# A selective scan with four convolutions: two packed tap matmuls, and u, z and dt sooner in the order

## The reference, cut to what matters

```
xz = einsum(x, in_proj_w); xi, z = split(xz)
xc = causal depthwise conv of xi over pixels, 4 taps
u = silu(xc + conv_b)
dt, B, C = split(einsum(u, x_proj_w)); delta = softplus(dt * dt_proj_w + b)
h = h * exp(delta * A) + delta * u * B        (one step per pixel, 16 states)
y = (h . C + u * D) * silu(z);  out = einsum(y, out_proj_w) + chunk
```

## Time and profile before

| | us |
|---|---|
| median of 3 runs | 8072.02 (8068.12 to 8075.87) |
| the profiled execution | 8083.31, of which the instructions span 8081.5 |
| TensorE busy | 6926.8 (86%) |
| VectorE busy | 6670.6 (83%) |
| ScalarE busy | 5321.7 (66%) |
| GpSimd busy | 5911.0 (73%) |

### The profile page before, as it was taken

One profiled execution on the slowest core, in us unless ns is written; L12 is line 12 of the kernel. 1 busy time (PEld: TensorE's weight loads), 2 busy tenths in 40 slices (PEclk: granted clock), 3 DMA queues, 4 the chain that ended last, 5 costly groups with the idle time before them and its releaser, 6 DMA issues. The chain is left out here.

```text
span 8081.5 us, 108343 instructions
## 1 busy us (share of the span) xinstructions
PE 6926.8 (86%) x31741; PEld 4163.9 (52%) x31741; DVE 6670.6 (83%) x9221; ACT 5321.7 (66%) x9423; POOL 5911.0 (73%) x5627
## 2 busy tenths in 40 slices
PE   8896877878888999999789999999789999996876
PEld 8893333333334555555435555555255555554665
DVE  6776989898989898999889999999898989894111
ACT  0135777777776778777777787777677787773221
POOL 0005989898988888888888888888888888884000
PEclk9998989898989999999989999999899999998999
DMA  9774666565667565656776566656865656565001
GB/s 169 166 179 123 179 166 180 166 178 163 181 173 191 162 164 159 164 165 162 184 194 169 159 166 163 165 157 164 208 172 162 167 159 166 161 164 137 2 2 32
DMA packets 1187366, 1261.38 MB, mean 156 GB/s; under 512 B 475904, under 2 KB 1172992, under 8 KB 1186816
## 3 DMA queue, kind: packets, MB, share of 16 engines
q1 hardware_dynamic: 950784, 1177.89, 54.9%
q10 hardware_dynamic: 236032, 77.08, 4.2%
HBM read 995.47 MB, written 181.59 MB: 146 GB/s over the span
## 5 line engine op out<-in xcount | busy, mean ns | idle before, releaser
L651 POOL TENSOR_TENSOR hs<-hs,bsp 128x448 f32<-128x448 f32 x3584 | 3718.2, 1059 | 411.5 <-DVE hs L641 401.2
L641 DVE TENSOR_TENSOR_SCAN hs<-da,hs,ps 128x448 f32<-128x448 f32 x3072 | 3491.6, 1137 | 0.0
L631 DVE TENSOR_TENSOR ps<-ps,bsp 128x448 f32<-128x448 f32 x3585 | 2200.3, 614 | 368.6 <-PE ps L615 367.9
L621 ACT ACTIVATE da<-da,nega 128x448 f32<-128x448 f32 x3588 | 2252.7, 661 | 51.5 <-issue 37.4
L856 PE MATMUL ps<-pv,ws 128*128 128x224 f32 x8800 | 1882.2, 359 | 218.1 <-DVE pv L920 122.4
L856 PEld LDWEIGHTS ps<-pv,ws 128*128 128x128 f32 x8800 | 1642.4, 190 | 502.3 <-DVE pv L920 202.7
L615 PE MATMUL ps<-stack,seld 96*128 96x448 bf16 x3587 | 1277.6, 370 | 349.4 <-DVE hs L641 260.9
L615 PEld LDWEIGHTS ps<-stack,seld 96*128 96x128 bf16 x3587 | 344.3, 98 | 1328.0 <-DVE hs L641 801.6
L920 DVE SCALAR_TENSOR_TENSOR pv<-ps,R 128x224 f32<-128x224 f32 x880 | 412.5, 469 | 734.6 <-PE ps L856 734.4
L662 PE MATMUL ps<-hs,wc 128*32 128x448 f32 x7200 | 964.2, 589 | 1.5 <-POOL hs L651 1.2
L422 PE MATMUL ps<-xn,wtap 128*128 128x448 f32 x1808 | 857.6, 577 | 9.7 <-ACT xn L526 9.7
(11 more groups left out here) (123 smaller groups left out, 8066.8 us busy)
## 6 DMA issues: line engine op xcount, KB each, us to landing
da<-delta_copy SPq DMA_DIRECT2D x3595, 224.0 KB, 3.8
stack<-parts SPq DMA_DIRECT2D x2700, 28.0 KB, 2.6
delta_copy<-dlt SPq DMA_DIRECT2D x225, 224.0 KB, 1.9
xin<-x_column_pairs SPq DMA_DIRECT2D x224, 145.0 KB, 3.5
x_column_pairs<-otile SPq DMA_DIRECT2D x225, 116.0 KB, 3.1
lnx<-in_x SPq DMA_DIRECT2D x115, 224.0 KB, 2.6
lny<-y_nchw SPq DMA_DIRECT2D x115, 224.0 KB, 2.8
xpad<-in_x SPq DMA_DIRECT2D x64, 392.0 KB, 7.1
```

Source lines behind the costliest of these rows:

```text
L621: a.activation(da[:, j % SLOTS, :], da[:, j % SLOTS, :], ACT.Exp, scale=nega[:, j:j + 1])\
L631: v.tensor_tensor(du, du, bsp[:, st.t % 2, 0, :], ALU.mult).then_inc(S["dbu_done"], 1)
L641: v.tensor_tensor_scan(hs[:, j, 1:T + 1], da[:, j % SLOTS, :], ps[:, DU_BANK + j % 4, 0:T], 0.0 if first else hs[:, j, T:T + 1], ALU.mult, ...
L651: g.tensor_tensor(hs[:, j, 0:T], hs[:, j, 1:T + 1], bsp[:, st.t % 2, 1, :], ALU.mult)\
```

## The change

The taps: `pack_pixels` (SyncE, two DMAs for each tile) copies the 64 rows of one image from xn into both halves of a new buffer xpack, the upper half one pixel further. One matmul then does two taps, so that `conv_tap` is two matmuls, and z reads xpack too. Its DMAs stand at unit 10 of SyncE, three tiles ahead, and wait for xn and for the reading of the buffer's last contents.

The order: on TensorE the taps end at unit 2, bc0 stands at 5 (before 6), dt at 6 (7), lnc at 7 (5), bc1 at 9 (8), lnv at 10 (9). On ScalarE silu's table, u, z and the other table stand at unit 4 (5), relu and cast0 behind them at 5 (4), bc0 at 6 (8), dt at 7 (9), lnc and cast1 at 8 (7), dt2 at 9, bc1 at 11, lnv at 12, clip at 13 (15). On GpSimd rest0 moves from 4 to 6, rest1 from 7 to 9, scale from 12 to 13, and delta_u from 15 to 14, ahead of the last product. The layer norm is done one tile sooner, and the last pair has none to prepare.

The blocks: one per tile, at unit 13 of TensorE, in a bank of the shared pair, read by VectorE at unit 15, loaded and stored at unit 5 of SyncE. Three are left for the tail. Steps are placed anew around them and no longer share a bank with blocks.

The rest: x3's borders are zeroed at the end of the second phase; work for tiles beyond the last is not issued.

```diff
-PE_AT = {0: ["tap0"], 1: ["last3", "tap1"], 2: ["tap2", "tap3"], 3: ["z"], 4: ["project"], 5: ["lnc"], 6: ["bc0"],
-         7: ["dt"], 8: ["sum0", "bc1"], 9: ["lnv"], 11: ["sum1"], 14: ["sum2"]}
+PE_AT = {0: ["tap0"], 1: ["last3"], 2: ["tap1"], 3: ["z"], 4: ["project"], 5: ["bc0"], 6: ["dt"], 7: ["lnc"],
+         8: ["sum0"], 9: ["bc1"], 10: ["lnv"], 11: ["sum1"], 13: ["blk"], 14: ["sum2"]}
 PE_US = {"tap": 0.9, "las": 0.95, "pro": 1.1, "z": 0.9, "lnc": 0.95, "lnv": 0.95, "bc0": 0.9, "bc1": 0.9, "dt": 0.9,
-         "sum": 0.95, "spread": 0.2, "skip": 0.9, "block": 2.25, "step": 1.9}
-ACT_AT = {0: ["prescale"], 4: ["relu", "cast0"], 5: ["silu", "u", "z", "exp"], 6: ["evacuate"], 7: ["lnc", "cast1"], 8: ["bc0"],
-          9: ["dt"], 10: ["dt2", "bc1"], 11: ["lnv"], 15: ["shift", "clip"]}
+         "sum": 0.95, "blk": 2.25, "spread": 0.2, "skip": 0.9, "block": 2.25, "step": 1.9}
+ACT_AT = {0: ["prescale"], 4: ["silu", "u", "z", "exp"], 5: ["relu", "cast0"], 6: ["evacuate", "bc0"], 7: ["dt"],
+          8: ["cast1", "lnc"], 9: ["dt2"], 11: ["bc1"], 12: ["lnv"], 13: ["clip"], 15: ["shift"]}
 DVE_AT = {3: ["gate"]}
-POOL_AT = {1: ["add_x"], 4: ["rest0"], 7: ["rest1"], 10: ["delta_log"], 12: ["scale"], 15: ["delta_u"]}
-SP_AT = {2: ["copy"], 8: ["part0"], 11: ["part1"], 13: ["part2"], 14: ["store"]}
+POOL_AT = {1: ["add_x"], 6: ["rest0"], 9: ["rest1"], 10: ["delta_log"], 13: ["scale"], 14: ["delta_u"]}
+SP_AT = {2: ["copy"], 8: ["part0"], 11: ["part1"], 10: ["pack"], 13: ["part2"], 14: ["store"]}
...
-            wtap = sb(m, "wtap", [P, 2, 4, P])
+            wtap = sb(m, "wtap", [P, 2, P])
+            xpack = sb(m, "xpack", [P, 2, T + 2])
...
-                self.has_ln = t < 4 or t >= 11
-                self.ln = p * KT + (t + 3 if t < 4 else t - 4)
-                self.ln_k = t + 3 if t < 4 else t - 11
-                self.ln_pair = p if t < 4 else (p + 1) % PAIRS
+                self.far_u = UB[ft]
+                soon, late = (3 if p else 4), ST - 4
+                self.has_ln = t < soon or t >= late and p + 1 < PAIRS
+                self.ln_pair = p if t < soon else (p + 1) % PAIRS
+                self.ln_k = t + KT - soon if t < soon else t - late
+                self.ln = self.ln_pair * KT + self.ln_k
...
+        FAR = ("tap0", "tap1", "u", "z", "dt", "dt2", "delta_log", "clip", "delta_u")
+        NEXT = ("bc0", "bc1", "cast0", "cast1", "rest0", "rest1", "copy", "part0", "part1", "part2")
+
+        def stands(st, name):
+
+            if name in FAR:
+                return st.far < TILES
+            if name in NEXT:
+                return st.next < TILES
+            return st.has_ln or name not in ("lnc", "lnv", "prescale", "relu", "shift", "add_x", "scale")
...
+                if name == "blk":
+                    if not BLOCKS_LEFT or tile < tile_of(*BLOCKS_LEFT[0]) + 2:
+                        continue
+                    BLOCK_AT[tile] = BLOCKS_LEFT.pop(0)
+                    TASK_LIST.append((name, BLOCK_NO[BLOCK_AT[tile]]))
+                elif not stands(st, name):
...
+            if back == "blk":
+                pe.wait_ge(D["cv_evac"], n + 2)
...
-                pe.wait_ge(S["xn_ready"], st.far_xn)
-            a = st.far_k * T + k
-            mm = pe.matmul(ps[:, TMP_BANK + bank, 0:T], wtap[:, st.far_s, k, :], xn[:, a:a + T],
-                           start=(k == 0), stop=(k == 3))
-            if k == 3:
+                pe.wait_ge(packed[st.far % 2], st.far // 2 * 32 + 32)
+            mm = pe.matmul(ps[:, TMP_BANK + bank, 0:T], wtap[:, k, :], xpack[:, st.far % 2, 2 * k:2 * k + T],
+                           start=(k == 0), stop=(k == 1))
+            if k == 1:
                 mm.then_inc(S["tmp_done"], 1)
+
+        def pack_pixels(sp, tile):
+
+            if tile >= 2:
+                sp.wait_ge(S["tmp_done"], Z_DONE[tile - 2])
+            s, k = tile % ST // KT, tile % KT
+            sp.wait_ge(S["xn_ready"], tile // ST * KT + k + 1)
+            for shift in range(2):
+                sp.dma_start(xpack[C * shift:C * shift + C, tile % 2, :],
+                             xn[C * s:C * s + C, k * T + shift:k * T + shift + T + 2]).then_inc(packed[tile % 2], 16)
...
-                    return pe.matmul(o, wcs("gate_in", st.far_s, P), xn[:, a:a + T], start=True, stop=True)
+                    return pe.matmul(o, wcs("gate_in", 0, P), xpack[:, st.far % 2, 2:T + 2], start=True, stop=True)
...
-            tail = []
-            for g in range(GROUPS):
-                for b in sorted(range(BLOCKS), key=lambda b: (tile_of(g, b), b)):
-                    ready = (tile_of(g, b) + 2) * UN + 8
-                    if ready > last - 4:
-                        tail.append(("block", g, b))
-                    else:
-                        place(("block", g, b), range(ready, min(ready + 16, last)))
...
+            with sp.Fori(0, PAIRS - 1) as i:
+                for b in range(2):
+                    sp.wait_ge(sa["split"], i * 2 + (b + 1))
+                    load_x(i + 1, b)
+            barrier(sp, 1)
...
             sp.wait_ge(D["zeroed"], 1)
             blank = hs[:, :, :].rearrange("p n f -> p (n f)")
             for rows in (0, H + 1):
                 sp.dma_start(x3[0:N, :, rows, :].rearrange("n p w -> p n w"),
...
-            sp.wait_ge(D["x3_zeroed"], 32)
-            barrier(sp, 1)
...
+                        if j == 5 and st.tile in BLOCK_AT:
+                            load_block(sp, *BLOCK_AT[st.tile])
+                        if j == 5 and st.tile - 1 in BLOCK_AT:
+                            keep_block(sp, *BLOCK_AT[st.tile - 1])
...
+                            elif name == "pack":
+                                if st.tile + 3 < TILES:
+                                    pack_pixels(sp, st.tile + 3)
...
+                            elif name == "blk":
+                                if st.tile in BLOCK_AT:
+                                    wait_bank(pe, st, name)
+                                    conv_block(pe, *BLOCK_AT[st.tile], TMP_BANK + BANK_NO[(st.tile, name)] % 2)
...
-            for s in range(2):
-                for k in range(4):
-                    ins = v.tensor_tensor(wtap[:, s, k, :], wps("conv_in", s, P), wps("taps", k, P), ALU.mult)
+            for k in range(2):
+                v.tensor_tensor(wtap[:, k, :], wps("conv_in", 0, P), wps("taps", k, P), ALU.mult)
...
+            v.wait_ge(D["x3_zeroed"], 32)
...
+                        if j == 15 and st.tile in BLOCK_AT:
+                            block_out(v, *BLOCK_AT[st.tile], TMP_BANK + BANK_NO[(st.tile, "blk")] % 2)
```

More of the change, by code:

```diff
@@ L726, in last_of @@
             return 55 * (d + 1)
[L728 removed]
+        LATE = {"dve": 2, "act": 6, "first": -3, "load": -8}
         FETCH, STEPS_FROM = 4 * UN, 6 * UN + 4
[L731 to L734 removed]
         def pe_work():
             out = []
[L739 removed]
+            for tile in range(TILES):
                 for j in range(UN):
@@ L840, in conv_block, with conv_step @@
             mm.then_inc(D["cv_done"], 1)
-        def conv_step(pe, G, m, alone=False):
+        def conv_step(pe, G, m):
             d = direction(m)
-            if not alone and PREVIOUS[("step", G, m)][0] == "block":
-                bank_free(pe, ("step", G, m))
             if m == last_of(d) - 54 + (d >= 2):
@@ L1073, in _ @@
             store(sp, tile, par, N - 1, k)
-            for j in range(LEAD["load"]):
-                sp.wait_ge(spread_in[j], (PAIRS * ST + 1) * 16)
-            for n in range(TILES * UN - LATE["keep"], TILES * UN):
-                if n in EV_AT and EV_AT[n][0] == "block":
-                    keep_block(sp, EV_AT[n][1], EV_AT[n][2])
+            keep_block(sp, *BLOCK_AT[TILES - 1])
             sp.wait_ge(S["y_summed"], TILES * 4 + 4)
-            sp.wait_ge(S["exp_done"], TILES * UN + LEAD["decay"] + 2)
             for k in range(NB):
@@ L1152, in _ @@
                     for j in range(UN):
-                        spread_du(pe, *unit(st, j + LEAD["du"]))
+                        if st.tile * UN + j + LEAD["du"] < TILES * UN:
+                            spread_du(pe, *unit(st, j + LEAD["du"]))
                         for name in PE_AT.get(j, ()):
+                            if not stands(st, name):
+                                continue
                             if name == "project":
@@ L1276, in _ @@
                     for j in range(UN):
-                        decay(a, *unit(st, j + LEAD["decay"]))
+                        if st.tile * UN + j + LEAD["decay"] < TILES * UN:
+                            decay(a, *unit(st, j + LEAD["decay"]))
                         for name in ACT_AT.get(j, ()):
+                            if not stands(st, name):
+                                continue
                             if name == "silu":
@@ L1305, in _ @@
                         e = event_at(st.tile, j, LATE["act"])
-                        if e is not None and e[0] == "step":
+                        if e is not None:
```

(3 more changed lines are left out.)

181 lines of the change are left out of this document (78 added, 103 removed).

## The result

The changed kernel is slower: 8348.22 us median (8340.72 to 8351.75, 4 runs) against 8073.94 of the kernel before beside it; the ratio is 1.0339 with a 95% interval of 1.0326 to 1.0352. The forecast was 7926 with a range of 7760 to 8120, faster. The profiled execution spans 8338.9 us against 8081.5, 257 more.

What follows compares the result with a forecast made beforehand. VectorE, GpSimd and TensorE were taken as near their limit, with the order deciding. Quiet norm −100, quiet plain +51, busy norm −108, busy plain +39, ends −20, −6, −1.9: 8072 − 146 = 7926 us, range 7760 to 8120.

Steps and rivals of the forecast that it cites:

- The loop: Gate, u and z, cast0, parts, landing, spread, block, next gate: 26.5 us, 26.6 with block_out's share.
- landing: The tile's last part DMA, from issue to arrival: 1.9 us taken, median 2.7, longest 3.2.
- the clock's 0.7: Block on TensorE partly at low clock behind its wait: 0.7 us per quiet plain tile, ends 0 and 2.3.
- Busy plain tiles: 78 tiles with steps and no layer norm: about 28.8 us each, +0.5, ends 0 to +1.5.
- the row: In busy plain tiles, a step's VectorE instruction like a drive, some 0.4 us, taking the clock term's place.
- Quiet norm tiles: Layer norm tiles without steps: 28.1 us each, −2.65; 38 of them counted, −100 us.
- GpSimd's 27.7: GpSimd's own work in a layer norm tile, 27.7 us, taken to bound quiet norm tiles over 27.1 for the chain.
- The second: Rival: last part lands later, packs at 0.65 and landing 2.7, 0.9 us more per tile: 8124 us, chance 0.24.
- The third: Rival: TensorE at 1.2 GHz for the block in all 74 quiet tiles, +118 us: 8044 us, chance 0.09.
- The first (hidden, 7728): Rival: parts land 1 us sooner and quiet plain tiles stay at 25.8 us: 7728 us, chance 0.15.
- their stall: In norm tiles, VectorE's 4.5 us of waits for a spread, claimed to go once u no longer waits for add_x.
- The start's gain: First phase: VectorE's 23.60 us wait for xpad shrinks to some 3 us as x3's borders move later: −20 us.

Runs made afterwards that it cites:

- The fillers: Changed kernel with 16 extra matmuls that compute nothing, on TensorE ahead of the next tile's first spread: 8155.50 us, ratio 1.0085.
- the mended one: Changed kernel with cast0 ahead of u, block at unit 12, packs at unit 14 and delta_u at unit 15: 7749.93 us, ratio 0.9585.
- its own run: Kernel before the change with only x3's zero borders moved to the end of the second phase: 8064.54 us, ratio 0.9976.

## Why the prediction was wrong, point by point

**The loop was right, its length was not.** The forecast named the loop and its links, and the trace has them in most tiles: u waits for the gate in 183 of 224, the spread for the parts in 220. For a quiet plain tile it said 27.3 us; the mean was 29.8. By its own terms (means over the quiet plain tiles of after): gate, u and cast0 4.3 (4.1 forecast); first issue to last 11.7 (11.3); landing 2.4 (1.9); from the spread to the next tile's start 5.6 (4.1 with the clock's 0.7); from there to the gate 5.7 (5.8).

**The step that failed** is the block's price, "so I take 0.7": the term for the clock in the loop, 0.7 us in quiet plain tiles, 0.4 in quiet norm and nothing in busy ones. I had set the ends at 0 and 2.3 and took a value near the low end because the quiet stretch of before had a clock of 0.88. But that 0.88 is a mean over TensorE's work, and in the kernel before the block stood ahead of the wait, and that wait was 1.6 us in quiet plain tiles, 0.7 in quiet norm and 0.1 in busy ones (means of TensorE's idle time before the spread). In the changed kernel the block stands behind the wait, which has grown to 4.9 us in quiet plain, 5.5 in quiet norm, 3.7 in busy plain and 2.7 in busy norm tiles (means). The block took 4.4, 4.3, 3.8 and 3.3 us there, where the forecast had 3.0, 2.7, 2.3 and 2.3 in its sum. Over all tiles that is an estimated 295 us, worked out from these means, of the 403 us between the forecast (146 less) and the profile (257 more). I had priced this as a rival at 8044 with a chance of 0.09, for quiet tiles alone; it came in busy ones too. The fillers gave back 193 us of it.

**Busy plain tiles** were the largest miss, +2.4 us each where I had +0.5: u to cast0 takes 3.8 us there instead of 2.95, since a step stands ahead of z on TensorE (in the tile at 6920, z's output kept ScalarE waiting 1.45 us), the gate comes 6.5 us after the tile's start instead of 5.8, and the block is slow as well. The stretch with a granted clock of 1.00 had made me leave the clock out of their sum. The sum itself was off too: 27.3 less the clock's 0.7, with 0.4 for the row, 0.5 and 1.0 make 28.5, and not 28.8, so its terms gave 0.3 less than it said.

**Quiet norm tiles**: −2.65 forecast, −0.7 measured (without the first four). I had let GpSimd's 27.7 bound them; the loop did, with relu in it and a block at 4.3 us.

**The first four tiles** had no place in the sum at all, +46. I had costed the packs as issues in SyncE's queue, and the wait in front of them (for xn) at nothing, though in the first pair, unlike the others, the layer norm of a tile is not done one tile sooner, and so ends five units behind the place of its pack.

**delta_u ahead of the last product** I had named, but only as a share of 0.5 us in busy plain tiles, and had put at nothing in quiet ones. In the changed kernel it was small (52 us). In the mended one it is 239.

**The rivals.** The second (longer by landing and packs) gave the right side, 8124, on the wrong mechanism: landing took 0.4 more in the mean of quiet plain tiles and nothing in busy ones (1.95), not 0.8. The third had the mechanism and a chance too small. None had the two together. The first (hidden, 7728) is near to what the mended kernel does: 7750.

**What was right**: norm tiles did lose their stall. ScalarE's waits for add_x, over the whole execution before and after:

```profile
ACT xres L515 <- POOL lny L509: 348.3, 110, 5.5
...
ACT xres L553 <- POOL lny L547: 2.8, 2, 1.6
```

dt, which had waited 142.5 us for lnx, no longer stands behind lnc. The start's gain was 17 us by its own run, 14.5 in the profile (20 forecast); the tail 2.4 (1.9).

What stays open: why cast0's place, worth 216 us in the changed kernel, is worth 4.5 in the mended one, is clear only in outline. There the loop with cast0 in it comes to 25.4 us by its terms, just under VectorE's 25.9. How much the packed taps bring by themselves, apart from blocks and the layer norm's shift, wasn't tried.

## What to carry to other kernels

A moved instruction is priced with what stands behind it: each of two misplaced tasks (a block one slot late, behind the instruction that waits; three steps of GpSimd ahead of the product that another engine waits for) cost over 200 us once all else was mended, and the reordering that they hid was worth 240. Where several links form a loop, taking them out singly misleads: cast0, block, packs and delta_u gave 216, 240, 183 and 52 us in the changed kernel, but cost 4.5, 213, 13 and 239 when put back into the mended one. Mend all, then take the mends out one by one. And put TensorE work into the wait, not behind it: here the same instructions took 4.69 us instead of 2.44 behind 5 us in which the engine had stood.

## What the runs showed of the hardware

- The same six matmuls took 2.44 us where TensorE had worked (granted clock 1.00) and 4.69 behind an idle time of 5.00 us (granted clock 0.50); with a burst of 16 matmuls in that idle time and 1.17 us left of it they took 2.44 (1.00), with 3.19 us left 3.91 (0.61).
- Sixteen more matmuls in each of 221 tiles, ahead of the wait, made the kernel 193 us faster.
- Two packs of 112.5 KB within the core took SyncE 1.18 us of issue in the median of 224 tiles and 1.99 in the tile at 1313; they landed 3.4 us after issue (median).
